# A fused attention and low-rank feed-forward layer: the low-rank term as a product of its own, and queries in 64-row products

## The chip, the cores and the metric

The kernel runs on one core of one Trainium2 chip. The metric is the device time of one execution in microseconds (us). Lower is better.

## What is computed

The input x has 2 sequences of 1024 tokens with 512 features. It is normalised over its features to xn. From xn come grouped-query attention s (32 query heads, 8 key and value heads, 16 features each, causal) and a gated feed-forward layer g. The output is x + s * g. Cut to what matters:

```python
q = xn @ Wq;  k, v = xn @ Wkv                    # 32 query heads, 8 groups
s = softmax(causal(q @ k.T) / sqrt(16)) @ v @ Wo + bo
def lora(x, w, a, b):                            # rank 16
    return x @ w.T + (x @ a.T) @ b.T
gate = lora(xn, gate_w, gate_a, gate_b)          # 512 -> 1376
up   = lora(xn, up_w, up_a, up_b)                # 512 -> 1376
g = silu(lora(silu(gate) * up, down_w, down_a, down_b))
out = x + s * g
```

All tensors are float32.

## The kernel before

**Split products.** A float32 factor is split into a rounded high part and a low part, both float32r, and a product is formed as high*high + high*low + low*high. `matmul_hi_lo` does that with three products over all 128 rows of the array (lines 289 to 291). Other places give each product only 64 rows: `hidden` (line 1018) and `changing_over` (line 1052) issue them in pairs, one in the upper half of the rows and one in the lower, each half into its own PSUM bank, and a second sweep (`cross`) goes over the same sum with the halves exchanged. A pair runs side by side. A profile row writes the rows and columns of the array that a product takes, as 128\*128, 64\*128 or 128\*32.

**Two programs woven into each engine's queue.** `attention()` runs in 16 rounds, one for each group and sequence, of 40 slots (`SLOTS`). A round has 48 score tiles `s` for the row maxima (line 1153, read by VectorE in `maximum`, lines 1730 and 1733; three banks), 40 transposed score tiles `st` (line 1172, two banks, one for each head of a pair), which ScalarE turns into `prob` by Exp (line 1449), causal masks by GpSimd (line 570), and context products `o` (line 1189). `background()` runs the rest: transposes of x (`turn`), projections (`proj`), values, the feed-forward units (`hidden`), then the down projection and the output. `interleave` hands out background work by steps: each unit has so many (`STEPS`), one step falls due per slot, and every engine follows the same count. `bank_order` is the order of the units. Two PSUM banks, `bank[0]` and `bank[1]`, serve the background; a unit takes one of them in turn, or both.

**Feed-forward weights.** For each block h of 128 hidden features (11 blocks, `NH`) and for gate and up (i = 0, 1), `fold(h, i)` transposes the raw weight (four products with the identity, line 993) and adds the low-rank product b*a into the same bank (four products, line 997). So the low-rank term goes into the weight. ScalarE rounds the result out of PSUM (`split_weight`, line 1278), VectorE subtracts for the low part (`low_weight`, line 1557). Then `hidden(h, c)` multiplies with the four chunks c of 512 tokens; ScalarE, VectorE and GpSimd form silu(gate)*up (lines 1289, 1571, 579, 581, 587). `fold_down` (lines 1032 and 1036) does the like for the down weights.

**Order in a period.** One h is a period of 40 slots in all queues: `hidden(h, 0)`, `hidden(h, 1)`, `fold(h + 1, 0)`, `fold(h + 1, 1)` (4 steps), one query projection of `AFTER` (4 steps), `hidden(h, 2)`, `hidden(h, 3)`. The last h has no folds.

**Start.** Before the first score tile stand eight turns, four projections (`LEADING`) and two values. During the first 40 slots, in which only `s` tiles and no Exp run, come the turns, projections and values of chunks 2 and 3, the first query projection of `AFTER` and `fold(0, i)`. Of the raw low-rank factors, `low_of_low_b` (line 1538) and `low_of_low_a` (line 1545) form low parts on VectorE, ahead of score maxima in its queue.

**Waits.** `scores_t` issues a pair of `st` products after one wait, which asks that both banks of the previous pair have been read by Exp.

## Time and profile before

| | us |
|---|---|
| median of 3 runs | 942.4 (938.22 to 943.74) |
| the profiled execution | 940.22 |
| its span, first to last instruction | 938.5 |
| TensorE busy | 894.9 (95%) |
| VectorE busy | 582.7 (62%) |
| ScalarE busy | 488.3 (52%) |
| GpSimd busy | 314.7 (34%) |
| transposes of `fold` (line 993), 88 products | median 273 ns |
| low-rank products of `fold` (line 997), 88 products | median 276 ns |

The span leaves 1.7 us of the profiled execution outside it. The profiled execution is one run; the median stands 2.2 us above it. PE is TensorE, DVE VectorE, ACT ScalarE, POOL GpSimd. Products overlap in the array, so the duration of one is longer than the distance to the next: the distances between starts say what a product takes of TensorE's time.

### The profile page before, as it was taken

The page shows a single profiled execution, that of the slowest core. Times are in us where ns is not written, and L with a number is a line of the kernel's source. Part 1 is how long each engine was busy: PE and PEld are TensorE (multiplying, and loading weights), DVE is VectorE, ACT ScalarE, POOL GpSimd, SP SyncE. Part 2 cuts the span into 40 slices and gives each one's busy share as a digit, 9 for nine tenths or more (in the row PEclk, how much of TensorE's full clock was granted, in tenths as well). Part 3 has the DMA queues.
Part 4 walks back from the last instruction along what each step waited for, and adds up shares of the span by engine and source line. Part 5 has one row for each costly group of instructions (what it writes and reads, how often), then busy time and mean ns, then how long its engine had stood idle before and what let it go on. Part 6 is the DMA issues. An engine that isn't in the chain of part 4 may idle for free.

```text
span 938.5 us, 21107 instructions
## 1 busy us (share of the span) xinstructions
PE 894.9 (95%) x8075; PEld 632.1 (67%) x8075; DVE 582.7 (62%) x1688; ACT 488.3 (52%) x990; POOL 314.7 (34%) x316
## 2 busy tenths in 40 slices
PE   3998999999999999999999999999899999999997
PEld 3755767676666666767666666654677777777885
DVE  6756666666666656566656565767666667660136
ACT  3513656565565656565656565656545455545211
POOL 4222235252525353535343443532011313130133
PEclk9979999999999999999999999997999999999999
DMA  9466343433334342424344434357475446434664
GB/s 292 160 197 186 103 131 97 120 98 113 111 104 122 93 135 72 141 68 138 80 121 107 120 89 134 80 141 209 143 221 158 155 142 178 153 110 123 214 209 141
DMA packets 133730, 129.20 MB, mean 138 GB/s; under 512 B 36176, under 2 KB 104368, under 8 KB 131360
## 3 DMA queue, kind: packets, MB, share of 16 engines
q1 hardware_dynamic: 133632, 127.87, 46.1%
q8 instruction: 65, 1.06, 0.5%
q14 instruction: 33, 0.27, 0.1%
HBM read 74.07 MB, written 53.22 MB: 136 GB/s over the span
## 4 chain that ended last, share of the span: by engine, by line
PE 88%; DVE 4%; ACT 2%; SPq 2%; issue 2%; DMA 2%; DVEq 0%; ACTq 0%
PE bank L1018 27%; PE o L1189 15%; PE bank L1052 12%; PE s L1153 10%; PE st L1172 8%; PE bank L289 4%; PE bank L290 4%; PE bank L291 4%; PE bank L993 1%; DMA ring<-in_L_attn_x 1%; PE bank L997 1%; ACT prob L1449 1%; SPq L933 1%; PE s L1160 1%; DVE junk L1730 1%
## 5 line engine op out<-in xcount | busy, mean ns | idle before, releaser
L1449 ACT ACTIVATE prob<-st 128x512 f32<-128x512 f32 (+1 forms) x640 | 323.2, 554 | 260.5 <-PE st L1172 260.0
L1730 DVE CUSTOM_DVE_ANT_0 junk<-s,mask 128x128 bf16<-128x128 f32 (+3 forms) x512 | 229.1, 487 | 67.2 <-PE s L1153 65.1
L1733 DVE TENSOR_REDUCE part_max<-s 128x1 f32<-128x512 f32 x256 | 164.1, 683 | 114.4 <-PE s L1153 114.3
L1153 PE MATMUL s<-k,q 64*128 64x512 f32 (+3 forms) x768 | 150.2, 378 | 10.7 <-DVE part_max L1730 5.3
L570 POOL TENSOR_SCALAR_AFFINE_SELECT prob<-prob 128x512 f32<-128x512 f32 x128 | 81.8, 651 | 218.4 <-ACT prob L1449 217.0
L1018 PE MATMUL bank<-x_hi,w_hi 64*128 64x512 f32 (+1 forms) x704 | 150.0, 412 | 2.5 <-DVE hid L1571 1.1
L1189 PE MATMUL o<-prob,v 128*32 128x512 f32 (+3 forms) x1536 | 145.0, 496 | 0.0
L1018 PE MATMUL bank<-x_lo,w_hi 64*128 64x512 f32 (+1 forms) x704 | 142.6, 391 | 0.0
L1018 PE MATMUL bank<-x_hi,w_lo 64*128 64x512 f32 (+1 forms) x704 | 142.1, 390 | 0.0
L1172 PE MATMUL st<-q,k 64*128 64x512 f32 (+3 forms) x768 | 130.3, 356 | 2.6 <-ACT prob L1449 1.8
L1052 PE MATMUL bank<-down_hi,late_context_hid_in 64*128 64x256 f32 x1056 | 113.3, 287 | 0.3 <-DVE y L1587 0.3
L1153 PEld LDWEIGHTS s<-k,q 64*128 64x128 f32 x768 | 78.7, 187 | 51.5 <-DVE part_max L1730 24.4
L579 POOL TENSOR_TENSOR tanh<-tanh,hid 128x512 f32<-128x512 f32 (+1 forms) x44 | 56.5, 1285 | 163.7 <-DVE hid L1571 163.7
L1052 PEld LDWEIGHTS bank<-down_hi,late_context_hid_in 64*128 64x128 f32 x1056 | 91.3, 188 | 16.1 <-issue 15.2
L1018 PEld LDWEIGHTS bank<-x_hi,w_hi 64*128 64x128 f32 (+1 forms) x704 | 69.2, 182 | 40.4 <-issue 30.6
L1172 PEld LDWEIGHTS st<-q,k 64*128 64x128 f32 x768 | 73.1, 186 | 29.0 <-issue 10.6
L1189 PEld LDWEIGHTS o<-prob,v 128*32 128x32 f32 x1536 | 39.7, 110 | 64.1 <-issue 58.0
L587 POOL TENSOR_TENSOR hid_lo<-hid,tanh_hid_hi 128x512 fp32r<-128x512 f32 (+1 forms) x44 | 56.8, 1292 | 72.0 <-ACT tanh_hid_hi L1306 72.0
L1052 PE MATMUL bank<-down_lo,late_context_hid_in 64*128 64x256 f32 x528 | 77.5, 281 | 0.1
L1018 PEld LDWEIGHTS bank<-x_lo,w_hi 64*128 64x128 f32 (+1 forms) x704 | 69.0, 182 | 12.5
L1018 PEld LDWEIGHTS bank<-x_hi,w_lo 64*128 64x128 f32 (+1 forms) x704 | 69.2, 183 | 7.8
L581 POOL TENSOR_TENSOR hid<-tanh,hid 128x512 f32<-128x512 f32 (+1 forms) x44 | 56.6, 1287 | 3.5
(148 smaller groups left out, 1088.7 us busy)
## 6 DMA issues: line engine op xcount, KB each, us to landing
late_context_hid_in<-scratch_hid SPq DMA_DIRECT2D x16, 1408.0 KB, 6.5
q<-scratch_q SPq DMA_DIRECT2D x60, 200.0 KB
scratch_hid<-tanh_hid_hi SPq DMA_DIRECT2D x40, 256.0 KB, 2.2
scratch_hid<-hid_lo SPq DMA_DIRECT2D x40, 256.0 KB, 2.5
scratch_o<-o_sb SPq DMA_DIRECT2D x32, 256.0 KB
scratch_q<-proj_hi SPq DMA_DIRECT2D x30, 256.0 KB
k<-scratch_k SPq DMA_DIRECT2D x30, 192.0 KB
x_again<-in_L_attn_x SPq DMA_DIRECT2D x16, 256.0 KB, 4.5
```

Of the source, the lines that this page charges most:

```text
L570: ins = pool.affine_select(out=blk, in_=blk, compare_op=ALU.is_ge, fill=0.0, base=0, pattern=[[0, REP], [1, P]], channel_multiplier=-1)
L579: pool.tensor_tensor(th[0:hp, n % 2], th[0:hp, n % 2], hid[0:hp, n % 2], ALU.mult).then_inc(tanh_used, 1)
L581: pool.tensor_tensor(hid[0:hp, n % 2], th[0:hp, n % 2], hid[0:hp, n % 2], ALU.add).then_inc(hid_done, 1)
L587: pool.tensor_tensor(hid_l[0:hp, n % 2], hid[0:hp, n % 2], hid_h[0:hp, n % 2], ALU.subtract)\
L1018: mm = pe.matmul(bank[i][0:hp, :], w_[half, h % 2, i, kt, 0:hp], x_[half, c, kt], start=not cross and kt == 0 and w_ is wh and x_ is xh, s ...
L1052: mm = pe.matmul(bank[i][:, COLUMNS[i]], lhs[half], rhs[half, COLUMNS[i]], start=not cross and n == 0 and m == 0, stop=cross == 1 and n == ...
L1153: pe.matmul(sb_[(p + odd) % S_BANKS][:, 0:wd], q[half, g % 2, h // 2, qt * P:(qt + 1) * P], k[half, g % 2, k0:k0 + wd], start=True, stop=T ...
L1172: mm = pe.matmul(st[odd][:, col:col + q1 - q0], k[half, i % 2, kt * P:(kt + 1) * P], q[half, i % 2, h // 2, q0:q1], start=True, stop=True)
L1189: mm = pe.matmul(ob[32 * h:32 * h + 2 * HD, q0 % C:q0 % C + q1 - q0], v[:, i % 3, kt].rearrange("p a e -> p (a e)"), prob[:, job % 3, h, c ...
L1449: nc.scalar.activation(prob[:, job % 3, h, 0:JOB_COLS[j]], st[at % ST_BANKS][:, 0:JOB_COLS[j]], ACT.Exp, scale=float(HD) ** -0.5).then_inc ...
L1730: ins = dve.tensor_tensor_reduce(junk[:, n % S_BANKS, 0:wd], bank_[:, 0:wd], mask[:, C - wd:C], 1.0, LOWEST, ALU.add, ALU.max, part[:, h, ...
L1733: ins = dve.tensor_reduce(part[:, h, qt, dst:dst + 1], bank_[:, 0:wd], AX.X, ALU.max)
```

## The change

- **The low-rank term leaves the weights.** `fold` is gone. The host hands over gate and up weights transposed, so that a raw tile arrives in the layout of `w_hi`. `low(i)` forms x*a for the gate and up factors together (32 columns) for two chunks at a time, eight float32 products, as i = 0 after the leading projections and i = 1 after the turns of chunk 3. The result is split and goes through DRAM (`store_x_a`, `load_x_a`) into `low_x_a`, whose rows 0 to 47 (gate) and 64 to 111 (up) hold high, low, high. In each `hidden(h, c)` one more pair of products, of 48 rows each, adds b times this to both banks (line 1108 of the changed kernel).
- **Weights are split from SBUF.** `round_weight` on ScalarE reads the raw tile; the subtraction moves from VectorE to GpSimd (`low_weight`). Both come two units before the block is used, beside `hidden(h, 2)` and `hidden(h, 3)`.
- **Query projections beside hidden units** (`BESIDE_HIDDEN`, 11 of them) go through `changing_over`: 48 products of 64 rows by 256 columns and both banks, in place of 12 of 128 rows by 512. They have 8 steps in place of 4 (the last one 4), so that a period keeps its 40.
- **Low parts of the small factors** leave VectorE: `low_of_low` on GpSimd takes the place of `low_of_low_b`; `low_of_low_a` has no successor.
- **One wait per score bank** in `scores_t`: the first product of a pair waits for its own bank, the second for its own.

Cut to its core:

```diff
+BESIDE_HIDDEN = AFTER[1:]
+QUERY_TILES = [[[0], [1], [2], [3]]] * 2
...
+QUERY_STEPS = [2 * KT] * (NH - 1) + [KT]
...
-STEPS = dict(turn=1, proj=KT, value=TT, fold=2, hidden=2 * KT, down_fold=2, rest=REST, down=NH + 1, out=KT)
+STEPS = dict(turn=1, proj=KT, value=TT, low=KT, hidden=2 * KT, down_fold=2, rest=REST, down=NH + 1, out=KT)
...
         yield "proj", c, blk
+    yield "low", 0, 0
     for c in range(2):
...
             yield "turn", c, k
+        if c == 3:
+            yield "low", 1, 0
...
-    for i in range(2):
-        yield "fold", 0, i
     for h in range(NH):
         for c in range(NCH):
             yield "hidden", h, c
             if c == 1:
-                if h + 1 < NH:
-                    for i in range(2):
-                        yield "fold", h + 1, i
                 yield "proj", *AFTER[SOON + h]
...
+EARLY = NUMBER_STEPS["proj", *AFTER[SOON - 1]] - FIRST_HIDDEN - LEAD
...
+            if kind == "proj" and (a, b) in BESIDE_HIDDEN:
+                return (p_left, BESIDE_HIDDEN.index((a, b)) + 1), (p_lo, projection(a, b) + 1)
...
+
+
+                pool.wait_ge(low_hi, 1)
+                pool.wait_ge(wq_lo, 3)
+                for half in range(2):
+                    at = slice(HALF_ROWS * half + 2 * R, HALF_ROWS * half + 3 * R)
+                    pool.tensor_tensor(b_gu[at], b_raw[at], b_gu[at], ALU.subtract).then_inc(low_lo, 1)
+                    pool.wait_ge(low_lo, half + 1)
+
+            def low_weight(h, i):
+                n, hp = 2 * h + i, rows[h]
+                pool.wait_ge(w_hi, n + 1)
+                pool.tensor_tensor(wl[:, h % 2, i, :, 0:hp], raw_tile(n)[:, :, 0:hp], wh[:, h % 2, i, :, 0:hp],
+                                   ALU.subtract).then_inc(w_lo, 1)
...
+                        low_of_low()
...
+                for i in range(2):
+                    low_weight(0, i)
...
                         done = at
                         if h or c:
                             low_hidden(*divmod(NCH * h + c - 1, NCH))
+                        if c >= 2 and h + 1 < NH:
+                            low_weight(h + 1, c - 2)
...
+            def load_x_a():
+                sp.wait_ge(x_a_stored, 2 * 2 * DMA)
+                for i in range(2):
+                    for j, part_ in enumerate((0, 1, 0)):
+                        row = HALF_ROWS * i + R * j
+                        sp.dma_start(low_x_a[row:row + R].rearrange("r (c t) -> r c t", c=NCH).bitcast(F32),
+                                     s["low"][part_, :, R * i:R * (i + 1)].rearrange("c r t -> r c t"))\
+                            .then_inc(x_a_landed, DMA)
...
-                    wait_filled(sp, ("fold", *divmod(before, 2)))
...
+                    sp.wait_ge(w_lo, before + 1)
...
                 out_ = take_bank(("proj", c, blk))
+                if (c, blk) in BESIDE_HIDDEN:
+                    cols = slice(blk * P, (blk + 1) * P)
+                    tiles = QUERY_TILES if (c, blk) != BESIDE_HIDDEN[-1] else OUT_STEPS
+                    yield from changing_over(
+                        ("proj", c, blk), lambda kt: [(wqh[:, kt, cols], xh[:, c, kt]), (wqh[:, kt, cols], xl[:, c, kt]),
+                                                      (wql[:, kt, cols], xh[:, c, kt])], tiles)
+                    return
...
-            def fold(h, i):
-                n = 2 * h + i
-                hp = rows[h]
-                pe.wait_ge(raw_landed[n % 8], DMA * (n // 8 + 1))
-                pe.wait_ge(low_lo, 2)
-                out_ = take_bank(("fold", h, i))
+            def low(i):
+
+
+                if i == 0:
+                    pe.wait_ge(low_landed, 2 * DMA)
+                pe.wait_ge(xT_copied, 2 * KT * (i + 1))
+                out_ = take_bank(("low", i, 0))
                 for kt in range(KT):
-                    pe.matmul(out_[:, kt * P:kt * P + hp], ring[0:hp, n % 8, kt * P:(kt + 1) * P], ident[0:hp, 0:hp],
-                              is_transpose=True, start=kt == 0, stop=False, skip_group_check=True)
-                yield 1
-                for kt in range(KT):
-                    mm = pe.matmul(out_[:, kt * P:kt * P + hp], a_gu[:, i, kt * P:(kt + 1) * P],
-                                   bT[:, i, h * P:h * P + hp], start=False, stop=kt == KT - 1, skip_group_check=True)
-                mm.then_inc(filled, 1)
-                yield 1
+                    for c in range(2):
+                        mm = pe.matmul(out_[GROUP * c:GROUP * (c + 1), :], a_raw[:, kt], xT[:, c, kt],
+                                       start=kt == 0, stop=kt == KT - 1)
+                    if kt == KT - 1:
+                        mm.then_inc(filled, 1)
+                    yield 1
 
...
+                        if kt == KT - 1 and not cross:
+                            if h == 0 and c == 0:
+                                pe.wait_ge(low_lo, 2)
+                                pe.wait_ge(x_a_landed, 6 * DMA)
+                            for i in range(2):
+                                at = head_rows(i, LOW_ROWS)
+                                mm = pe.matmul(bank[i][0:hp, :], b_gu[at, h * P:h * P + hp], low_x_a[at, c * C:(c + 1) * C],
+                                               start=False, stop=False)
                         if kt == KT - 1:
                             mm.then_inc(filled if cross else crossed, 1)
                         yield 1
...
-                if at >= ST_BANKS:
-                    pe.wait_ge(exp_done, at)
                 for kt, q0, q1, col in JOBS[j]:
                     for odd in range(2):
+                        if at >= ST_BANKS and kt == JOBS[j][0][0]:
+                            pe.wait_ge(exp_done, at + odd - 1)
...
+                if (c, blk) in BESIDE_HIDDEN:
+                    for i in range(2):
+                        ins = nc.scalar.activation(projected(n)[0][:, COLUMNS[i]], bank[i][:, COLUMNS[i]], ACT.Copy)
+                else:
+                    ins = nc.scalar.activation(projected(n)[0], bank_of(key)[:, :], ACT.Copy)
+                ins.then_inc(p_hi, 1)
...
-            def split_weight(h, i):
-                key = ("fold", h, i)
...
-                wait_filled(act, key)
...
-                nc.scalar.activation(wh[:, h % 2, i, :, 0:hp],
-                                     bank_of(key)[:, :].rearrange("p (k h) -> p k h", k=KT)[:, :, 0:hp],
-                                     ACT.Copy).then_inc(w_hi, 1)
+            def round_weight(h, i):
+                n, hp = 2 * h + i, rows[h]
+                if n == 0:
+                    wait_filled(act, ("value", NCH - 1, 0))
+                    act.wait_ge(xT_lo_late, 2 * KT)
+                act.wait_ge(raw_landed[n % 8], DMA * (n // 8 + 1))
+                nc.scalar.activation(wh[:, h % 2, i, :, 0:hp], raw_tile(n)[:, :, 0:hp], ACT.Copy).then_inc(w_hi, 1)
...
+                        yield WEIGHT_STEPS
+                        if c >= 2 and h + 1 < NH:
+                            round_weight(h + 1, c - 2)
...
-                dve.tensor_tensor(lo, bank_of(key)[:, :], hi, ALU.subtract).then_inc(p_lo, 1)
...
+                if (c, blk) in BESIDE_HIDDEN:
+                    for i, read in enumerate((p_left, p_lo)):
+                        dve.tensor_tensor(lo[:, COLUMNS[i]], bank[i][:, COLUMNS[i]], hi[:, COLUMNS[i]], ALU.subtract).then_inc(read, 1)
+                else:
+                    dve.tensor_tensor(lo, bank_of(key)[:, :], hi, ALU.subtract).then_inc(p_lo, 1)
...
-            def low_weight(h, i):
...
-                dve.wait_ge(w_hi, 2 * h + i + 1)
-                dve.tensor_tensor(wl[:, h % 2, i, :, 0:hp],
-                                  bank_of(key)[:, :].rearrange("p (k h) -> p k h", k=KT)[:, :, 0:hp],
-                                  wh[:, h % 2, i, :, 0:hp], ALU.subtract).then_inc(w_lo, 1)
...
+    for name in ("gate_w", "up_w"):
+        arrays[f"in_L0_ffn_{name}"] = np.ascontiguousarray(arrays[f"in_L0_ffn_{name}"].T)
```

The order of instructions shows two places. The first is TensorE's queue in the middle of a period, from the last context products ahead of the folds to the first work behind the first pair of `st` and `s` tiles. Before:

```order
L1189 MATMUL o<-prob,v 32x512 x3
L993 MATMUL bank<-ident,ring 128x128 [waits gate_read,up_read,low_lo_done,raw_landed4]
L993 MATMUL bank<-ident,ring 128x128 x3
L997 MATMUL bank<-bT,low_a 128x128 x4
L1172 MATMUL st<-q,k 128x512 [waits exp_done]
L1172 MATMUL st<-q,k 128x512
L1153 MATMUL s<-k,q 128x512 [waits s_read]
L1153 MATMUL s<-k,q 128x512
L993 MATMUL bank<-ident,ring 128x128 [waits gate_read,up_read,low_lo_done,raw_landed5]
```

And now (L1142 is the product of `changing_over`, L1260 and L1241 are the `st` and `s` tiles):

```order
L1277 MATMUL o<-prob,v 32x512 x3
L1142 MATMUL bank<-x_hi,wq_hi 128x256 [waits gate_read,up_read,wq_lo,xT_lo]
L1142 MATMUL bank<-x_hi,wq_hi 128x256
L1142 MATMUL bank<-x_lo,wq_hi 128x256 x2
L1142 MATMUL bank<-x_hi,wq_lo 128x256 x2
L1142 MATMUL bank<-x_hi,wq_hi 128x256 x2
L1142 MATMUL bank<-x_lo,wq_hi 128x256 x2
L1142 MATMUL bank<-x_hi,wq_lo 128x256 x2
L1260 MATMUL st<-q,k 128x512 [waits exp_done] x2
L1241 MATMUL s<-k,q 128x512 [waits s_read]
L1241 MATMUL s<-k,q 128x512
L1142 MATMUL bank<-x_hi,wq_hi 128x256 x2
```

Where two folds stood now stand 64-row products of the query projection, which has come forward by four steps; between context products and context products every product has 64 rows.

The second is GpSimd's queue between `finish` of one hidden unit and `finish` of the next (`tanh` and `hid` are its two products, `prob` the causal mask). Before:

```order
L587 TENSOR_TENSOR hid_lo<-hid,tanh_hid_hi 128x512 [waits hid_done,hid_hi_done]
L570 AFFINE_SELECT prob<-prob 128x4x128 [waits exp_done]
L579 TENSOR_TENSOR tanh<-tanh,hid 128x512 [waits up_read,gate_read]
L581 TENSOR_TENSOR hid<-tanh,hid 128x512 [waits tanh_used]
L570 AFFINE_SELECT prob<-prob 128x4x128 [waits exp_done]
```

And now:

```order
L621 TENSOR_TENSOR hid_lo<-hid,tanh_hid_hi 128x512 [waits hid_done,hid_hi_done]
L646 TENSOR_TENSOR w_lo<-ring,w_hi 128x512 [waits w_hi_done]
L604 AFFINE_SELECT prob<-prob 128x4x128 [waits exp_done]
L613 TENSOR_TENSOR tanh<-tanh,hid 128x512 [waits up_read,gate_read]
L615 TENSOR_TENSOR hid<-tanh,hid 128x512 [waits tanh_used]
```

A subtraction of a weight tile, which waits for ScalarE's rounding, stands behind `low_hidden`, ahead of a mask and of the next `finish`. It does so twice in each period but the last.

## Rows read from the trace of the kernel before

**Rows 1.** The page: head, busy time, and the maxima of 512 columns (busy, mean ns).
```profile
span 938.5 us, 21107 instructions
...
PE 894.9 (95%) x8075; PEld 632.1 (67%) x8075; DVE 582.7 (62%) x1688; ACT 488.3 (52%) x990; POOL 314.7 (34%) x316
...
L1733 DVE TENSOR_REDUCE part_max<-s 128x1 f32<-128x512 f32 x256 | 164.1, 683 | 114.4 <-PE s L1153 114.3
```

**Rows 2.** Waits of TensorE for Exp: us in total, times, longest.
```profile
PE st L1172 <- ACT prob L1449: 1.8, 4, 1.0
```

**Rows 3.** Stretches: us, busy of PE, PEld, DVE, ACT, POOL, then PEclk, DMA share, GB/s.
```profile
43.00:49.00 6.00, 3.96 (x24) 2.38 (x22) 5.92 (x10) 4.51 (x9) 4.25 (x3) 0.97 0.55 174
50.00:62.00 12.00, 12.00 (x30) 6.53 (x28) 5.29 (x21) 0.60 (x1) 2.69 (x3) 0.50 0.62 178
250.00:560.00 310.00, 308.99 (x2645) 208.29 (x2642) 197.41 (x608) 184.68 (x378) 129.23 (x127) 1.00 0.38 106
634.00:643.00 9.00, 7.37 (x47) 4.26 (x47) 7.42 (x24) 6.16 (x14) 5.60 (x6) 0.98 0.49 127
643.00:652.00 9.00, 9.00 (x49) 4.83 (x48) 6.95 (x27) 4.53 (x9) 0.63 (x1) 0.50 0.82 238
```

**Rows 4.** Timeline of TensorE, one period: start us, us, operation.
```profile
211.55 0.39 PE L1018 MATMUL bank<-x_lo,w_hi 64*128 64x512 f32 x2
211.78 0.39 PE L1172 MATMUL st<-q,k 64*128 64x512 f32 x2
...
214.27 1.92 PE L1189 MATMUL o<-prob,v 128*32 128x512 f32 x16
216.13 0.66 PE L993 MATMUL bank<-ident,ring 128*128 128x128 f32 x4
216.54 0.64 PE L997 MATMUL bank<-bT,low_a 96*128 96x128 f32 x4
217.12 0.50 PE L1172 MATMUL st<-q,k 64*128 64x512 f32 x2
217.45 0.40 PE L1153 MATMUL s<-k,q 64*128 64x512 f32 x2
...
219.66 0.50 PE L289 MATMUL bank<-x_hi,wq_hi 128*128 128x512 f32 x1
...
221.25 0.49 PE L1172 MATMUL st<-q,k 64*128 64x512 f32 x2
...
223.48 0.50 PE L1172 MATMUL st<-q,k 64*128 64x512 f32 x2
...
264.90 0.66 PE L993 MATMUL bank<-ident,ring 128*128 128x128 f32 x4
```

**Rows 5.** Timeline of TensorE: six pairs of 64x256 products, first, and what follows.
```profile
800.01 0.31 PE L1052 MATMUL bank<-wo_hi,ctx_hi 64*128 64x256 f32 x2
...
800.72 0.42 PE L1172 MATMUL st<-q,k 64*128 64x512 f32 x2
```

**Rows 6.** Timeline of ScalarE in the same period: two Exp.
```profile
217.72 1.08 ACT L1449 ACTIVATE prob<-st 128x512 f32<-128x512 f32 x2
```

**Rows 7.** Timeline of GpSimd: one subtraction of a 128x512 tile.
```profile
210.30 1.30 POOL L587 TENSOR_TENSOR hid_lo<-hid,tanh_hid_hi 128x512 fp32r<-128x512 f32 x1 [1.23 <-ACT tanh_hid_hi L1306]
```

**Rows 8.** Timeline of TensorE during fold_down: two neighbouring st pairs.
```profile
655.23 0.50 PE L1172 MATMUL st<-q,k 64*128 64x512 f32 x2 [0.18 <-ACT prob L1449]
...
656.89 0.50 PE L1172 MATMUL st<-q,k 64*128 64x512 f32 x2
```

**Rows 9.** Timeline of TensorE at the start: two score pairs that waited.
```profile
47.60 0.38 PE L1153 MATMUL s<-k,q 64*128 64x256 f32 x2 [1.17 <-DVE part_max L1730]
...
90.61 0.44 PE L1153 MATMUL s<-k,q 64*128 64x384 f32 x2 [2.37 <-DVE part_max L1733]
```

**Rows 10.** Timeline of VectorE at the start: the low parts of b and a.
```profile
43.72 3.51 DVE L1538 TENSOR_TENSOR bT<-prob,bT 32x688 fp32r<-32x688 f32 x3
...
88.53 1.21 DVE L1545 TENSOR_TENSOR low_a<-prob,low_a 32x1024 fp32r<-32x1024 f32 x1 [2.78 <-ACT low_a L1261]
```

221 lines of the change are left out of this document (118 added, 103 removed).

## The prediction

> **What bounds the kernel now.** I read the page first. TensorE is busy for 894.9 of 938.5 us, and VectorE, ScalarE and GpSimd are far behind it [rows 1]. Then the stretches: between 250 and 560 us, where `hidden`, `fold` and the query projections run beside attention, TensorE is busy for 308.99 of 310.00 us at full clock [rows 3]. The waits agree: `st` waits for Exp only 1.8 us in all [rows 2]. So in the middle what counts is how long TensorE's own queue takes, instruction by instruction. That is seen in the timeline, in distances between starts and not in durations. A pair of 64x512 products takes 0.23 us (211.55 to 211.78), and a pair of 64x256 half of it: six pairs take 0.71 us (800.01 to 800.72), 0.118 each [rows 4, 5]. Where a 64-row product follows one of 128 rows or stands ahead of it, the distance is 0.33 in place of 0.23 (217.12 to 217.45): a change between the two costs 0.10 on either side of it, and `fold` and the projections make such changes around each `st` and `s` pair [rows 4].
>
> There are two further losses in the rows. At the start score pairs wait for maxima (1.17 us at 47.60, 2.37 us at 90.61), while VectorE works on the low parts of b and a [rows 9, 10]. And the clock stands at 0.50, the lower of its levels (1.2 GHz), from 50 to 62 us and again from 643 to 652 us; before it fell TensorE had been busy for 3.96 of 6.00 and for 7.37 of 9.00 us [rows 3].
>
> **The change, part by part.**
>
> *The folds and the query projection in a period.* From the first fold to the first `st` pair behind the projection is 7.35 us (216.13 to 223.48) [rows 4]. In it lie two folds, twelve 128x512 products, three `st` pairs and three `s` pairs (512, 384 and 512 columns wide). In its place will stand 24 pairs of 64x256 at 0.118 = 2.84 us, three `st` pairs at 0.23 = 0.69, `s` pairs of 0.23 + 0.17 + 0.23 = 0.63, and 0.11 for the change behind the context products: 4.27 us. The `st` pair at 223.48 loses its 0.11 as well. That is 7.35 - 4.27 + 0.11 = 3.19 us, ten times: 31.9 us off. Slots keep their count, so nothing else moves.
>
> *What that stretch then waits for.* Two Exp take 1.08 us and begin 0.60 us behind their `st` pair (217.12, 217.72), 0.40 in the new stretch, where nothing is drained ahead of it (a row of such a pair lasts 0.39) [rows 4, 6]. So they end 1.48 us behind it, and with the hand-over about 1.5. The next pair comes 0.23 + 0.23 + 0.71 = 1.17 us behind the last. Its first product may now go with its bank free, but its second waits 0.35 us. From then on Exp runs without a gap and the pairs wait about 0.1 each. I take 0.5 us a period, 5.0 us given back. The floor is 0; the ceiling is the pace of `fold_down`, where neighbouring `st` pairs stand 1.66 us apart (655.23, 656.89) [rows 8]: 0.49 us more for each of three, 15 us in all. Nearest is the sum from Exp, since it is this stretch's own arithmetic.
>
> *The low-rank pair in each unit.* 44 units take one more pair of 512 columns: 44 x 0.23 = 10.1 us on, if 48 rows go like 64. For this speaks that the 96-row products of line 997 follow the 128-row ones of line 993 after 0.41 us, four transposes' own time, with nothing added (216.13, 216.54) [rows 4].
>
> *The last period* has no folds. Its twelve products take 4 x 0.79 = 3.18 us (219.66 to 221.25 is six of them with their first change), and some 0.8 us more of changes around them, against 2.84: 1.1 us off.
>
> *The first two folds* go: 0.99 us each (216.13 to 217.12) [rows 4], and 0.5 of changes: 2.5 us off.
>
> *Low parts at the start.* `low_of_low_a` held VectorE with its maxima behind it; the 2.37 us at 90.61 go. What replaces it in ScalarE's queue is two roundings, which no maximum waits for. With `low_of_low_b` gone (3.51 us for three of four), the 1.17 us at 47.60 go [rows 9, 10]. Off: 3.5 us. On GpSimd the same low parts stand ahead of the low parts of chunk 3, which are needed far later.
>
> *The products x*a.* Sixteen context products of 128\*32 take 1.86 us (214.27 to 216.13) [rows 4], so four 32-column tiles side by side take 0.465. A pair of `low` takes at least that, as its columns are streamed once: 8 x 0.465 = 3.7 us on. If the two don't run side by side it is 7.4. I take 3.7.
>
> *The clock at the start.* From 50 to 62 us all runs at half speed. If the clock holds, these 12 us take 6 or 7, as the maxima then set part of the pace. In the new order TensorE has less of a hole before it: the waits just named are gone, and `low(0)` pushes 1.9 us of dense work between the projections and the turns. I take it that the clock holds: 5.0 us off; bounds 0 and 6.
>
> *One wait per score bank* gives at most the 1.8 us of [rows 2], of which part is in places as tight as before: 0.5 us off.
>
> *At nothing:* ScalarE's rounding is the same 22 instructions. GpSimd gains 22 subtractions of 1.30 us (210.30) [rows 7], twice in a period of 48.8 us (216.13 to 264.90) [rows 4], in which it is busy for two fifths of the time (129.23 of 310.00) [rows 3]. Behind them in its queue stand a mask and `finish`. The weights are wanted only in the next period, and the tile loads on SyncE that wait for them stand half a unit later. A mask delayed by 1.3 us is wanted by a context product two slots after the last Exp of its job, some 2.4 us (48.8 / 40 each). If that cover is gone it costs up to 1.3 us at a mask, 26 us at most for 20 of them.
>
> **Sum:** -31.9 + 5.0 + 10.1 - 1.1 - 2.5 - 3.5 + 3.7 - 5.0 - 0.5 = -25.7 us, from the profiled execution's 940.2: **914.5 us**. The median of the runs is 942.4, so as a difference it is 2.7%.
>
> **The rivals.**
> - *The clock falls at the start as before.* For it: the hole between the values and the projections is still there, as ScalarE sets the pace of the turns. 5 us more: 919.5. I count it with the forecast's surroundings, chance 0.25.
> - *The query stretch is bound by Exp and maxima.* VectorE has 1.37 us for a pair of maxima of 512 columns (2 x 0.683) [rows 1], and TensorE only 1.17. Then it goes at the pace of `fold_down`, 15 us in place of 5: 924.5. For it: [rows 8] show just such a stretch. Against it: context products of 1.86 us stand on both sides, so VectorE begins with an empty queue. Chance 0.20.
> - *TensorE's columns alone decide.* No wait in the stretch: 909.5, and with some of the waits of [rows 2] gone 908. Chance 0.13.
> - *The 48-row pair doesn't go with its neighbours* (slower or equal). Each stands between 64-row products. If 48 rows are a setting of their own, each pays a change on both sides, 2 x 0.20, and its two products go one after the other, 0.23: 44 x 0.63 = 27.7 us on, 942. It decides from 25.7 / 44 = 0.58 us per unit. The Trainium skill (TensorEngine Tiling (Array Packing), "Key Properties") says "Changing tiling mode (not just tile) drains the TensorE" and lists row tiles of 128, 64 and 32 only; by that page 48 rows would be a 64-row tile, and 96 no other than 128, with which the 0.41 us above agrees. Chance 0.05.
> - *The clock falls in the query stretches* (slower). They hold half of the columns of a `hidden` stretch of as many slots, and the clock did fall in `fold_down`. At half speed for 9 us in each of ten periods [rows 3] it costs 45 us: 959. It decides from six periods. Against it: here TensorE would still work for 4.27 of 4.8 us. The Trainium skill (TensorE: Matmul & The Clock Gate, "What's actually happening") has the clock set by how busy the array has been; the two falls in the rows agree. Chance 0.04.
> - *GpSimd holds others up.* 20 masks delayed past their cover by the whole of a subtraction are the 26 us above, half of them 13: 927 to 940. For it: the subtraction stands straight ahead of a mask. Against it: no wait of TensorE for a mask is in the rows. Chance 0.05. The Trainium skill (SBUF — State Buffer, "SBUF: two separate sides") says that GpSimd and a VectorE operation with two SBUF inputs shut each other out for a whole instruction. By that rule the small split of the maxima, whose inputs are both in SBUF, could stand 1.3 us behind each of the 22 new subtractions, 28 us at the worst and next to nothing where the row maxima come back early; it speaks against the change, and no row here prices it.
>
> The forecast itself, with the clock held and short waits, has 0.28.
>
> **How the numbers follow.** A measurement of this kernel tells about 0.5% (5 us) from no change. From 908 to 925 lie the forecast, the first three rivals and most of what is between them: 0.86. The range that leaves out the two slow ends and takes in the doubled `low` (3.7 more) is 905 to 928. Faster by over 0.5% holds in all cases but the 48-row pair (same, 0.05) and the clock in each period (slower, 0.04): 0.91.
>
> **What would show it.** Six 64x256 pairs of the query projection in 0.71 us, and neighbouring `st` pairs there some 1.2 to 1.3 us apart; the stretch from the end of the context products to the next `st` behind the projection near 4.8 us. The pair of line 1108 between two 64x512 pairs at 0.23. A period of 48.8 - 3.2 + 0.5 + 0.9 = 47.0 us. No 2.37 us wait before the first hidden unit. PEclk at 1.00 between 50 and 62 us. The prediction fails if the 48-row pair shows gaps, if PEclk falls in each period, if VectorE or Exp hold the stretch, or if TensorE waits for masks.

## The result, and the profile after

The changed kernel takes 934.0 us (median of 8 runs, 931.33 to 935.92), the kernel before 940.8 in the same rounds (938.06 to 943.74): ratio 0.993, 95% interval 0.991 to 0.995. It is faster by 0.7%, 6.8 us, where I had forecast 2.7%, and the time lies above my range. The profiled execution has a span of 933.6 us against 938.5 [rows 1].

The page of the changed kernel, its head and busy time:

```profile
span 933.6 us, 21793 instructions
...
PE 885.7 (95%) x8415; PEld 641.2 (69%) x8415; DVE 576.6 (62%) x1674; ACT 488.9 (52%) x1002; POOL 345.4 (37%) x340
```

TensorE's busy time fell by 9.2 us, its instructions rose by 340. The stretches of [rows 3], and with them 102 to 108 us (columns: us, busy time of PE, PEld, DVE, ACT, POOL, then PEclk, DMA share, GB/s):

```profile
43.00:49.00 6.00, 5.84 (x44) 4.49 (x43) 5.05 (x20) 3.51 (x7) 1.75 (x2) 1.00 0.52 166
50.00:62.00 12.00, 10.38 (x53) 7.05 (x53) 9.73 (x26) 1.56 (x3) 9.73 (x5) 1.00 0.59 166
102.00:108.00 6.00, 2.93 (x13) 0.93 (x15) 0.51 (x4) 0.74 (x2) 1.23 (x2) 0.54 0.65 171
250.00:560.00 310.00, 308.62 (x2903) 219.46 (x2903) 201.10 (x623) 190.53 (x396) 148.73 (x143) 1.00 0.41 110
```

The clock holds from 50 to 62 us, as forecast. A new stretch is slow: from 102 to 108 us the granted clock is 0.54 and TensorE is busy for 2.93 of 6.00 us. The middle is as full as it was. What TensorE waits for in the first 125 us (total, times, longest), the first is in no such list of the kernel before:

```profile
PE s L1241 <- DMA q<-scratch_q: 6.6, 1, 6.6
PE s L1241 <- DVE part_max L1812: 2.9, 3, 1.5
...
PE bank L1077 <- ACT xT L1318: 1.3, 1, 1.3
```

The first row is the largest new thing in the trace. The chain that ended last, between 76 and 112 us (start us, us, what), leads back from it:

```profile
88.90 0.42 SPq L768
...
89.83 0.59 SPq L749
...
91.08 7.94 DMA scratch_k<-proj_hi
...
100.31 4.72 DMA q<-scratch_q
105.07 0.47 PE s L1241 x2
...
107.73 1.58 PE bank L1099 x6
```

And SyncE's queue in the same stretch:

```profile
83.37 1.31 SPq L749 DMA_DIRECT2D scratch_q<-proj_hi  x2
84.72 0.56 SPq L749 DMA_DIRECT2D scratch_q<-proj_lo  x1
85.33 4.46 SPq L768 DMA_DIRECT2D low_x<-scratch_low  x6
89.83 0.59 SPq L749 DMA_DIRECT2D scratch_k<-proj_hi  x1
90.46 0.57 SPq L749 DMA_DIRECT2D scratch_k<-proj_lo  x1
91.08 0.57 SPq L749 DMA_DIRECT2D scratch_k<-proj_hi  x1
99.07 0.79 SPq L949 DMA_DIRECT2D k<-scratch_k  x2
99.90 1.48 SPq L952 DMA_DIRECT2D q<-scratch_q  x4
```

The six loads of x times low_a (line 768) stand between the queries' stores and the keys' stores. The last store of keys lands 7.94 us after its issue begins, then k and q are loaded, then the scores of head group 1 can start, at 105.07 us. In the kernel before, SyncE's queue has the last store of keys and the load of k at:

```profile
83.95 0.68 SPq L692 DMA_DIRECT2D scratch_k<-proj_hi  x1
...
90.57 1.08 SPq L874 DMA_DIRECT2D k<-scratch_k  x2
```

There k is loaded 6.6 us behind the last store, here 8.0. The first hidden unit starts at 99.29 us in the kernel before and at 107.66 here.

The query stretch and the 48-row pair, TensorE's timeline, one period (to be held against [rows 4]):

```profile
221.07 1.92 PE L1277 MATMUL o<-prob,v 128*32 128x512 f32 x16
222.93 0.39 PE L1142 MATMUL bank<-x_hi,wq_hi 64*128 64x256 f32 x2
...
223.74 0.39 PE L1260 MATMUL st<-q,k 64*128 64x512 f32 x2
...
224.91 0.89 PE L1260 MATMUL st<-q,k 64*128 64x512 f32 x2
...
226.37 0.39 PE L1260 MATMUL st<-q,k 64*128 64x512 f32 x1
...
228.59 1.92 PE L1277 MATMUL o<-prob,v 128*32 128x512 f32 x16
...
234.08 0.43 PE L1108 MATMUL bank<-low_x,low_b 48*128 48x512 f32 x2
234.31 0.43 PE L1260 MATMUL st<-q,k 64*128 64x384 f32 x4
```

From the end of the context products to the next ones is 5.66 us (222.93 to 228.59), 8.02 before (216.13 to 224.15). The 48-row pair goes with its neighbours: 0.23 us from its start to the next.

### The profile page after: what moved, and what is told of

Read it like the earlier page. It is cut to its first block, busy times and chain, and to the rows that moved or that the text cites. A ratio compares the mean times of both kernels' runs of the same rounds, so it can differ in the third digit from the quotient of the medians.

```text
span 933.6 us, 21793 instructions
## 1 busy us (share of the span) xinstructions
PE 885.7 (95%) x8415; PEld 641.2 (69%) x8415; DVE 576.6 (62%) x1674; ACT 488.9 (52%) x1002; POOL 345.4 (37%) x340
## 4 chain that ended last, share of the span: by engine, by line
PE 86%; DVE 4%; DMA 3%; SPq 2%; ACT 2%; issue 2%; DVEq 0%; ACTq 0%
PE bank L1099 28%; PE bank L1142 15%; PE o L1277 14%; PE s L1241 9%; PE st L1260 8%; PE bank L306 3%; PE bank L307 2%; PE bank L308 2%; DMA sums<-scratch_o 1%; PE bank L1108 1%; PE bank L1077 1%; PE bank L1062 1%; SPq L968 1%; DMA scratch_k<-proj_hi 1%; PE bank L1122 1%
## 5 line engine op out<-in xcount | busy, mean ns | idle before, releaser
L1241 PE MATMUL s<-k,q 64*128 64x512 f32 (+3 forms) x768 | 157.6, 376 | 15.4 <-DMA q<-scratch_q 6.6
L1260 PE MATMUL st<-q,k 64*128 64x512 f32 (+3 forms) x768 | 141.7, 347 | 1.0 <-ACT prob L1543 0.5
L1241 PEld LDWEIGHTS s<-k,q 64*128 64x128 f32 x768 | 80.9, 187 | 54.0 <-DVE part_max L1809 22.7
L1142 PE MATMUL bank<-down_hi,late_context_hid_in 64*128 64x256 f32 x1056 | 114.2, 287 | 0.3 <-DVE y L1669 0.3
L1142 PEld LDWEIGHTS bank<-down_hi,late_context_hid_in 64*128 64x128 f32 x1056 | 93.3, 188 | 15.8 <-issue 15.0
L1260 PEld LDWEIGHTS st<-q,k 64*128 64x128 f32 x768 | 85.1, 187 | 19.6 <-ACT prob L1543 8.3
L1142 PE MATMUL bank<-down_lo,late_context_hid_in 64*128 64x256 f32 x528 | 79.1, 281 | 0.0
```

Of the source, the lines that this page charges most:

```text
L1142: mm = pe.matmul(bank[i][:, COLUMNS[i]], lhs[half], rhs[half, COLUMNS[i]], start=not cross and n == 0 and m == 0, stop=cross == 1 and n == ...
L1241: pe.matmul(sb_[(p + odd) % S_BANKS][:, 0:wd], q[half, g % 2, h // 2, qt * P:(qt + 1) * P], k[half, g % 2, k0:k0 + wd], start=True, stop=T ...
L1260: mm = pe.matmul(st[odd][:, col:col + q1 - q0], k[half, i % 2, kt * P:(kt + 1) * P], q[half, i % 2, h // 2, q0:q1], start=True, stop=True)
```

## Where the time went, by parts

I cut both programs in each period at the same slot: at the first product behind the context products that follow `hidden(h, 1)`. In the kernel before that is the first fold, in the changed kernel the first query product. (The first query product of the kernel before would be no such mark, since two folds stand ahead of it: 216.13 and 219.66 in [rows 4].) There are eleven marks; the first ten are nine periods apart. In us of the profiled executions, last column the mean of the nine:

| kernel | first mark | tenth mark | span | period |
|---|---|---|---|---|
| before | 118.67 | 557.50 | 938.5 | 48.76 |
| changed | 128.06 | 554.11 | 933.6 | 47.34 |

The program behind the first mark is 14.3 us shorter, the start 9.4 us longer. The middle gave 1.42 us a period, forecast 1.8 (48.8 to 47.0). From the tenth mark to the end it is 379.5 us against 381.0, 1.5 shorter, where my terms for that part make 2.4 (3.19 - 0.5 for the last stretch with folds, 1.1 for the last period, less six pairs of 0.23). Most of the miss is in the start. One execution says only so much of it: four kernels with the same start (the changed one and experiments 4, 8 and 11) reach the first mark at 128.06, 126.45, 125.28 and 125.32 us, mean 126.3; two with the start of before (that kernel and experiment 12) at 118.67 and 121.12, mean 119.9. So the start costs about 6.4 us more than before. Four terms of my sum (-2.5, -3.5, +3.7, -5.0) had taken 7.3 off it, and two 48-row pairs give 0.5 back. That is a miss of some 13 us, of 19 in all.

How the wait at the scores of head group 1 comes about is seen from the way of the last keys, in us of each profiled execution: when their low part is ready on VectorE, when their last store is issued, when the load of k is issued, when the scores start, and how long TensorE halts for them. The experiments are those of the next section.

| kernel | low part ready | last store | load of k | scores | halt |
|---|---|---|---|---|---|
| before | 82.69 | 83.95 | 90.57 | 97.84 | none |
| before, two waits (experiment 12) | 82.24 | 83.50 | 90.75 | 100.17 | none |
| changed | 88.38 | 91.08 | 99.07 | 105.07 | 6.55 |
| same start, experiment 4 | 85.63 | 88.33 | 96.43 | 102.86 | 7.12 |
| same start, experiment 8 | 84.62 | 87.60 | 95.46 | 101.44 | 6.68 |
| same start, experiment 11 | 84.72 | 86.80 | 95.61 | 101.56 | 6.70 |
| experiment 1 | 86.09 | 87.72 | 94.91 | 101.90 | 5.68 |
| experiment 2 | 85.29 | 87.40 | 95.68 | 102.13 | 6.72 |
| experiment 5 | 87.22 | 88.85 | 94.71 | 101.29 | 3.94 |
| experiment 9 | 80.96 | 83.33 | 90.26 | 96.33 | none |
| experiment 10 | 78.34 | 81.65 | 89.37 | 95.41 | 1.58 |

With the changed start (mean of its four kernels) k is loaded 6.0 us later than with the start of before (mean of two): the keys are ready 3.4 us later, their last store is issued a further 1.35 us later, and the load of k comes 1.25 us later behind it. TensorE for its part is through with its other work 3 us earlier than before, and halts.

## The experiments

All in rounds with the kernel before; ratios are to it, with their 95% interval. Its median was 940.8 us beside the changed kernel, 941.0 in experiments 1 to 4, 938.6 in 5 to 8 and 939.6 in 9 to 12, so between these groups the ratios compare better than the times.

**1. The six loads behind the last keys' stores.** The edit, in SyncE's order:

```diff
                     store_projection(*BESIDE[c])
-                    if c == 3:
-                        load_x_a()
                     yield STEPS["proj"]
                     store_projection(c, KEYS_BLOCK)
+                    if c == 3:
+                        load_x_a()
```

> One edit to the changed kernel: on SyncE the six loads of x times low_a stand behind the three stores of the last keys instead of ahead of them. Theory A (the order in SyncE's queue makes TensorE wait): the last keys are stored about 4.5 us earlier, TensorE's wait of 6.55 us for q<-scratch_q at 105.07 falls under 1.5 us, and with it the stretch at half clock behind it; the first hidden unit starts at 99 to 102 us instead of 107.66, and the time is 925 to 928.5 us (ratio to before 0.983 to 0.987). Rival B (the transfers themselves contend, whatever their order): the wait stays over 4 us and the time is 931 to 935. Rival C: the loads are now late for the first hidden unit, which waits over 2 us for them: 929 to 932.

Measured: 931.4 us, ratio 0.990 (0.988 to 0.992), against 0.993 for the changed kernel. SyncE's queue:

```profile
87.72 0.56 SPq L749 DMA_DIRECT2D scratch_k<-proj_hi  x1
88.34 5.58 SPq L768 DMA_DIRECT2D low_x<-scratch_low  x6
94.91 0.78 SPq L949 DMA_DIRECT2D k<-scratch_k  x2
```

TensorE, in the same kernel:

```profile
101.90 0.47 PE L1241 MATMUL s<-k,q 64*128 64x128 f32 x2 [5.68 <-DMA q<-scratch_q]
```

The last store is issued 3.4 us earlier (87.72 in place of 91.08), but 2.3 of that are the execution, in which the keys were ready earlier (86.09 in place of 88.38); the order in the queue gives 1.1. With the loads right behind it the store lands 7.13 us after its issue begins, and the wait is still 5.68 us. Rival B holds: the order of issue is a small part. The intervals of the two ratios overlap, and the first hidden unit starts at 104.49 us, where experiments 4, 8 and 11, which leave the start as it is, have 105.46, 104.03 and 104.16.

**2. A quarter of the products x times low_a.** The edit, in `low`:

```diff
-                    for c in range(2):
+                    for c in range(2 * (kt == KT - 1)):
                         mm = pe.matmul(out_[GROUP * c:GROUP * (c + 1), :], a_raw[:, kt], xT[:, c, kt],
-                                       start=kt == 0, stop=kt == KT - 1)
+                                       start=True, stop=True)
```

> The changed kernel with only one of the four row blocks of the product x times low_a (8 instead of 32 products; it leaves out three quarters of that sum, all else stays). Theory: these products are a plain cost on TensorE at the start, 0.9 us for a pair of products at full clock and more at half clock, so that 7 us go: first hidden unit at 100 to 101.5 us, time 926 to 928.5 (ratio 0.984 to 0.987), and the granted clock at 66 to 78 us is 1.0. Rival: the start is set by the chain of stores and loads behind SyncE, not by TensorE's own work: the wait for q<-scratch_q grows instead, and the time is 931 to 934.

Measured: 932.4 us, ratio 0.991 (0.988 to 0.993). Three quarters of 32 records at 0.23 us went, 5.6 us of TensorE's time at full clock, and 1.6 us were won, which the rounds hardly tell from nothing. The first hidden unit starts at 104.73 us, and the last keys are ready at 85.29, no earlier than with all the products (84.62 and 84.72 in experiments 8 and 11). The time is the rival's and the wait stays, 6.72 us, though it doesn't grow. But my theory also asked for a granted clock of 1.00 from 66 to 78 us, and it was 0.72, as in the changed kernel; in experiments 4, 8 and 11 it is 1.00 there. So part of the work that went may have come back as lower clock, and this run doesn't separate the two.

**3. The small subtraction on GpSimd moved.** The low parts of low_b are computed behind the last query weights (`low_of_low()` moved below `low_query_weights(3)`, with its own wait for them).

> The changed kernel with GpSimd's subtraction for the low parts of low_b (2 instructions of 3.16 us) moved from 53.6 us to behind the last query weights, at about 72 us. Theory (GpSimd holds VectorE up while it runs them): the third instruction of the split of the maxima, 3.12 us at 56.87 us, is under 0.5 us, and the 1.53 us wait of a score product at 61.33 is gone; time 932 to 933 (ratio 0.991 to 0.992), if no other VectorE instruction is held up at 72 to 79 us. Rival: the long subtraction has another cause and stays at about 3 us.

Measured: 931.7 us, ratio 0.990 (0.988 to 0.992). VectorE's timeline in the changed kernel:

```profile
56.66 0.17 DVE L1823 CAST neg_pad<-neg_max 128x16 fp32r<-128x16 f32 x1
56.87 3.12 DVE L1825 TENSOR_TENSOR neg_pad<-neg_max,neg_pad 128x16 fp32r<-128x16 f32 x1
```

GpSimd's beside it, the same kernel:

```profile
53.63 6.32 POOL L640 TENSOR_TENSOR low_b<-prob,low_b 16x1376 fp32r<-16x1376 f32 x2
```

And VectorE's in this one:

```profile
55.76 0.17 DVE L1823 CAST neg_pad<-neg_max 128x16 fp32r<-128x16 f32 x1
55.97 0.18 DVE L1825 TENSOR_TENSOR neg_pad<-neg_max,neg_pad 128x16 fp32r<-128x16 f32 x1
```

The same instruction on 128x16 elements takes 3.12 us or 0.18. In the changed kernel it ends at 59.99 us, and the two subtractions of GpSimd end at 59.95: it stood still for the whole of the second one. In all nine profiled kernels with the subtraction at this place one instruction of this split lasts 3.10 to 3.13 us; in the three with it moved neither does. In experiment 2 it was the one before, a copy, at 54.97, and GpSimd ended at 58.05. The Trainium skill (SBUF — State Buffer, "SBUF: two separate sides") says the pair of ports that the two share is locked for a whole instruction and the loser blocks; the trace agrees, with 3.12 against 0.18. I had cited this rule for the 22 new subtractions in the middle and not looked at the start, where a subtraction is 3.16 us long. TensorE's wait for maxima at 61.33 us fell from 1.53 to 0.32 (at 60.45). That is not yet time won: in experiment 8, with the subtraction at its old place, the same score product starts 4.65 us behind that copy on VectorE (55.88 to 60.53), and here 4.69 behind it (55.76 to 60.45), with a wait of 1.30 us for queries shortly before. So the hold-up is shown, and a cost to the program is not; the ratio overlaps with the changed kernel's.

**4. Query products of 128 rows again.** `BESIDE_HIDDEN = []`, with the same eight steps.

> The changed kernel with the ten query projections between the hidden units as products of 128 rows again, in the same eight steps. Theory (changes between 64-row and 128-row products and the time the array drains are what the 64-row products save): the stretch of 5.66 us becomes 6.5 to 7.0, 0.9 to 1.3 us in each of ten periods: 943 to 947 us (ratio 1.002 to 1.007). Rival (the 64-row products give nothing, since the time goes to waits for Exp and score banks): 933 to 937.

Measured: 940.9 us, ratio 1.000 (0.998 to 1.002). The stretch is 6.40 us (222.36 to 228.76) in place of 5.66, and the period 47.93 us in place of 47.34. The 64-row products give 0.6 to 0.7 us a period, 6 to 7 us in all; I expected 0.9 to 1.3, and the time lies between my range and the rival's. Their gain is clear, its size was too high.

**5. The six loads behind the values' stores too.** As in the first experiment, one place further down, so that k and q are loaded ahead of them.

> One edit to the changed kernel: the six loads of x times low_a (0.79 MB) stand in SyncE's order behind the last keys' and values' stores, and so behind the loads of k and q for the second head group too. Theory A2 (it is the bytes of the six loads in the DMA engines, and not only their 4.5 us of issuing, that hold up keys and queries; in the run with the loads right behind the keys the last store still took 6.6 us to land): that store lands in 3 to 4.5 us, the wait for q<-scratch_q falls under 1.5 us, the first hidden unit starts at 97 to 100.5 us, and the time is 924 to 927.5 us (ratio 0.982 to 0.9855). Rival: the landing is slow for another reason (other stores and loads in the same stretch): the wait stays over 4 us, 930 to 933.

Measured: 930.8 us, ratio 0.992 (0.990 to 0.994), which these rounds don't tell from the first experiment, nor from the changed kernel (0.991 to 0.995). The last store lands 5.80 us after its issue begins, in place of 7.94, and the wait is 3.94 us. The wait is 6.55 to 7.12 us in the four kernels with the loads ahead of the keys, and falls with each step by which the loads' 0.79 MB go back, to 5.68 and 3.94 in one execution each. But most of it stays: theory A2 is a part too. Left over is that the last keys are projected late and too little work stands behind them.

**6. Both.** Experiments 3 and 5 together.

> The edit of the run before and GpSimd's subtraction for low_b moved behind the last query weights, together. If the two losses at the start are independent and nothing new waits: 1.5 to 2.5 us below the run before, 922.5 to 925.5 (ratio 0.980 to 0.984), granted clock 1.0 at 66 to 78 us and at 96 to 108 us. Rival: they share one slack, and it is within 1 us of the run before.

Measured: 928.6 us, ratio 0.990 (0.988 to 0.992), span 927.0. The median is 2.1 us below the run before, as for independent losses, but above my range; the intervals overlap, so the sum is likely and not shown. The clock didn't come back everywhere: 0.72 from 66 to 72 us and 0.72 and 0.71 between 96 and 108.

**7. Without the 48-row pairs.**

```diff
-                            for i in range(2):
-                                at = head_rows(i, LOW_ROWS)
-                                mm = pe.matmul(bank[i][0:hp, :], b_gu[at, h * P:h * P + hp], low_x_a[at, c * C:(c + 1) * C],
-                                               start=False, stop=False)
```

> The changed kernel without the 44 pairs of 48-row products (it leaves out the low-rank term of gate and up, and keeps the work that prepares it). My price for them: 44 times 0.23 us, 10.1 us: 922.5 to 925.5 (ratio 0.981 to 0.984). Rival (the pair changes the array's mode or waits, and costs over 0.3 us each): under 921. Rival (the units wait for something else behind the first half, so the pairs are partly free): 927 to 931.

Measured: 923.4 us, ratio 0.983 (0.981 to 0.986), 10.6 us below the changed kernel (9.1 by the ratios); the period is 46.55 us, 0.79 less, so 0.20 for each of its four pairs. The price of 10.1 us was right.

**8. One wait for both score banks.**

```diff
+                if at >= ST_BANKS:
+                    pe.wait_ge(exp_done, at)
                 for kt, q0, q1, col in JOBS[j]:
                     for odd in range(2):
-                        if at >= ST_BANKS and kt == JOBS[j][0][0]:
-                            pe.wait_ge(exp_done, at + odd - 1)
```

> The changed kernel with one wait for both score banks of a pair again, as before the change. My price for that step is 0.5 us: 933.5 to 935.5, so no difference that five rounds can tell. Rival (where TensorE reaches the scores before Exp is done, in the query stretches, the first product of a pair fills 0.1 to 0.2 us each time): 936 to 939.

Measured: 938.1 us, ratio 0.998 (0.996 to 1.000), where the changed kernel has 0.993 (0.991 to 0.995). The rival holds. TensorE's waits for Exp from 125 us on (total, times, longest) in this kernel:

```profile
PE st L1260 <- ACT prob L1543: 9.1, 33, 1.0
```

The changed kernel:

```profile
PE st L1260 <- ACT prob L1543: 0.5, 1, 0.5
```

And one place in a query stretch with one wait:

```profile
222.91 0.28 PE L1142 MATMUL bank<-x_hi,wq_lo 64*128 64x256 f32 x2
223.42 0.50 PE L1260 MATMUL st<-q,k 64*128 64x512 f32 x2 [0.23 <-ACT prob L1543]
223.76 0.34 PE L1241 MATMUL s<-k,q 64*128 64x384 f32 x2
223.94 0.28 PE L1142 MATMUL bank<-x_hi,wq_hi 64*128 64x256 f32 x2
...
225.09 0.49 PE L1260 MATMUL st<-q,k 64*128 64x512 f32 x2 [0.29 <-ACT prob L1543]
```

The 0.23 us shown as a wait is not all: from the last query pair to the `st` pair is 0.51 us where 0.12 would do, as between two query pairs, and the pair loses 0.11 at its end. Three times a period this makes a stretch of 6.38 us (221.05 to 227.43) against 5.66. The `st` pairs stand 1.56, 1.67 and 1.67 us apart here (221.86, 223.42, 225.09, 226.76), the pace of `fold_down` in [rows 8].

**9. The second product of low_a behind the last keys.** On top of experiment 5, `low(1)` stands behind the projection of the last keys, on all engines, in place of ahead of the two projections:

```diff
-                    if c == 3:
-                        yield from low(1)
                     yield from project(*BESIDE[c])
                     yield from project(c, KEYS_BLOCK)
+                    if c == 3:
+                        yield from low(1)
```

> The changed kernel with the six loads behind the last values' stores as in the run before, and with the second product of x times low_a behind the projection of the last keys instead of ahead of the two projections (on all engines). Theory A3 (what binds is the chain from the last keys' projection over store and load to the first scores of head group 1, about 12 us, and TensorE has less work behind that projection than it had): the projection is ready 3 to 5 us earlier and the product covers the wait: the wait for q<-scratch_q is under 1 us, the wait for xT of 1.32 us is gone, first hidden unit at 98 to 100.5 us, 925.5 to 928.5 us (ratio 0.984 to 0.9875). Rival: the six loads become the late ones and the first half of the first hidden unit ends in a wait of over 2 us for low_x: 929 to 932.

Measured: 927.8 us, ratio 0.987 (0.984 to 0.990). TensorE's waits for loads in the start, and the scores of head group 1:

```profile
PE bank L1108 <- DMA low_x<-scratch_low: 2.4, 1, 2.4
PE s L1241 <- DMA q<-scratch_q: 2.1, 1, 2.1
```

```profile
96.33 0.33 PE L1241 MATMUL s<-k,q 64*128 64x128 f32 x2
```

The 2.1 us for queries lie at 58.62 us, in the first head group, where the other kernels wait up to 2.01 us too; the scores of head group 1 start at 96.33 without a wait. The first hidden unit starts at 97.79 us, ten earlier than in the changed kernel and six to eight earlier than in experiments 4, 8 and 11, and halts in its middle at 101.9 us for the loads, which land last. Both A3 and its rival show, and the time is that of A3: the chain of the keys is covered, and the loads are the late ones, for 2.36 us. Behind this wait the clock is at its lower level again: 64x512 pairs stand 0.43 us apart (105.47, 105.90) in place of 0.23.

**10. The same and the small subtraction moved.**

> The run before with GpSimd's subtraction for low_b behind the last query weights as well. 1.5 to 2.5 us below it if the two are independent: 923.5 to 926.5 (ratio 0.981 to 0.985); within 1 us of it if they share a slack.

Measured: 927.4 us, ratio 0.986 (0.983 to 0.989), span 924.8, first mark 120.16, period 47.27. It is within 0.5 us of the run before, as I gave for a shared slack; experiment 3 can't show a gain of its own for this move either, so what they share stays open. The unit still halts 1.83 us for the loads. This is the best version, 1.4% below the kernel before and 0.7% below the changed one. Its first mark is still no earlier than that of the kernel before (118.67, and 121.12 in experiment 12), where my sum had it 6.8 us earlier.

**11. Experiments 4 and 8 together.**

> The changed kernel with 128-row query products and one wait for both score banks, both undone together. Each alone costs 4 to 7 us. If they work only together (with one wait the faster stretch runs into Exp, with 128-row products Exp is never late): no more than either alone, 939 to 943 us (ratio 0.998 to 1.003), and hardly a wait of st for prob. If they add up: 944 to 948.

Measured: 942.4 us, ratio 1.003 (1.001 to 1.005). The two edits don't add up: 942.4 is within the 939 to 943 that I gave for that. TensorE waits for Exp only here and there:

```profile
PE st L1262 <- ACT prob L1545: 1.6, 3, 1.0
```

**12. One wait per bank in the kernel before.**

> The kernel before with nothing changed but one wait per score bank. If that step only pays where the query products are short: no difference (ratio 0.998 to 1.002). If it pays by itself: 3 to 6 us faster (0.9935 to 0.997).

Measured: 938.6 us, ratio 1.000 (0.997 to 1.002). The period is 48.75 us, as before.

The marks of the last group, which hold the middle apart from the start:

| kernel | first mark | tenth mark | period |
|---|---|---|---|
| before | 118.67 | 557.50 | 48.76 |
| before, two waits | 121.12 | 559.88 | 48.75 |
| changed, 128-row queries and one wait | 125.32 | 558.22 | 48.10 |
| changed, 128-row queries, two waits | 126.45 | 557.86 | 47.93 |
| changed, 64-row queries, one wait | 125.28 | 556.22 | 47.88 |
| changed | 128.06 | 554.11 | 47.34 |
| changed, no 48-row pairs | 124.92 | 543.90 | 46.55 |

Removing the folds gives 48.76 - (48.10 - 0.79) = 1.45 us a period. On the 48.10, the two waits alone give 0.17, the 64-row queries alone 0.22, both 0.76: they work together, and nearly half of what they give is there only with both.

## Why the prediction was wrong, step by step

- **The step that failed is the start: -2.5 for the first two folds, -3.5 for the low parts, +3.7 for the products x*a and -5.0 for the clock, where the start came out 6.4 us longer.** Under the products x*a I wrote only their columns on TensorE, and the folds I counted as pure gain. What that left out is the way of the last keys through DRAM. The change moves these keys back by `low(0)` and `low(1)`, puts six loads of 0.79 MB ahead of them in SyncE's queue, and takes two folds, 2 us of cover, from behind them. The result is a wait of 6.55 to 7.12 us in every kernel with this start, and the lower clock behind it. Of the 6.0 us by which k is loaded later, 3.4 are keys that are ready later and 2.6 the queue and the landing. Experiments 1, 5 and 9 move nothing but the order around it. Only the last, which puts `low(1)` behind the keys, takes the wait away: its ratio, 0.984 to 0.990, doesn't overlap with the changed kernel's 0.991 to 0.995. That the folds covered part of it is argued from their place; no run puts them back.
- **The products x*a were mis-sized:** forecast 3.7 us for both, measured 3.6 for the first alone. The products in the trace of the changed kernel (records, durations in ns, min/median/max):

```profile
L1077 PE MATMUL bank<-xT,prob x32: 592/604/1061, 34.2 to 75.9; 128*32 128x512 f32 x32
```

The products of the values, the other plain float32 ones:

```profile
L1062 PE MATMUL bank<-wkv,xT x128: 272/275/377, 37.8 to 93.0; 128*128 128x128 f32 x128
```

Each of the 16 products of 512 columns has two records, and a record lasts 0.604 us where a pass of 512 columns lasts 0.39: 0.21 more, which is 512 columns at 2.4 GHz. So a product here streams its columns four times. The records stand 0.23 apart, so the two tiles do run side by side, as I took it. I had taken the price from context products, whose operands are rounded to float32r, for a product of plain float32. The fitting row was in the kernel before, the products of the values:

```profile
84.87 2.05 PE L980 MATMUL bank<-wkv,xT 128*128 128x128 f32 x16
```

So 16 records of 128 columns take 2.05 us, 0.26 for a product's two, where 128 columns at 2.4 GHz are 0.053. The Trainium skill (FP8 and Floating Point Precision, "TensorE Precision Notes") gives true FP32 four passes through the array; the trace agrees. At half clock, as for part of `low(1)` in the changed kernel, the same takes longer still: eight of its records 3.63 us against 1.91 in experiment 5.
- **The clock at the start:** it held from 50 to 62 us, as I took it, but the 5.0 us were not won, since it was low elsewhere: 0.81 from 62 to 80 us and 0.54 from 102 to 108. The first belongs to this execution, for experiments 4, 8 and 11 have 1.00 there. The second stands in all of them (0.50 to 0.54), behind the wait for the keys. The fall that I priced varies too: with the start of before, experiment 12 has 0.72 from 50 to 62 us and 0.59 from 92 to 98. I had priced a fall as something that goes; it has to be asked where the next hole will be.
- **Low parts at the start:** the waits of [rows 9] went. "On GpSimd the same low parts stand ahead of the low parts of chunk 3, which are needed far later" looked at the queue behind them and missed VectorE beside them: a new wait of 1.53 us for maxima stands at 61.33. What it costs the program isn't shown (experiment 3).
- **Folds and query projection:** 24 pairs at 0.118 came as forecast (the first six in 0.81 with the change, six others in 0.71). The stretch is 5.66 us between context products, where my figures make 5.3 (8.02 - 3.19 + 0.5). The period gave 1.42 instead of 1.8, and this stretch is 0.33 of the difference.
- **What that stretch waits for:** I took 0.5 us a period, of waits. Without any the stretch would be 4.83 us by my figures (8.02 - 3.19). It is 5.66, so they are 0.83, and with one wait for both banks 6.38, so 1.55. In the changed kernel the list of waits shows only 0.5 us for the whole program, since TensorE rarely stands still as a whole. The time is in the pairs, whose two products no longer start together (226.37, one record in place of two).
- **One wait per score bank** was the worst-sized term of the middle: forecast 0.5 us in all, measured 0.54 a period and 4 to 5 us in the time, because I read its worth from the waits of the kernel before. There it is worth nothing (experiment 12), and with 128-row query products 0.17 a period. It is worth the 0.54 only in the short stretch that another part of the change makes.
- **The rivals:** the clock did fall at the start, elsewhere than before; the query stretch isn't bound by Exp or maxima at the pace of `fold_down` (its `st` pairs stand 1.17 and 1.46 us apart, not 1.66), but with one wait for both banks it is (experiment 8), and the 15 us of that rival fit the 1.55 a period; the clock stays at 1.00 in the periods. The time lies in the range that I gave the rival of GpSimd's masks, 927 to 940, and its cause is another. No rival had the way of keys and queries through DRAM.
- **The 48-row pair** was right in mechanism and size (10.1, measured 10.6). **GpSimd's 22 subtractions** cost TensorE next to nothing in the middle: no wait for a mask, none for weights. They do hold VectorE up, as my last rival had it: between 125 and 560 us its 18 small subtractions of the maxima (line 1825) take 15.4 us in place of 12.0. But TensorE's waits for maxima from 125 us on are 4.5 us against 4.1, so the maxima come early enough. **The last period** was to give 1.1 us less. Its stretch took 5.22 us (601.67 to 606.89) against 5.41 (606.84 to 612.25), 0.2 less: it ends in a wait for VectorE's low part of the projection, 1.22 us against 0.90.

What stays open: why one execution of the same start takes up to 2.8 us more than another (128.06 against 125.28), of which the clock is the visible part; and how the 2.6 us of queue and landing divide, since the loads' issues and their bytes move together in experiments 1 and 5.

## What to carry to other kernels

When work is taken out of TensorE's queue, look for the transfer that it covered: keys and queries were on their way through DRAM beneath the two folds. When work is put in, look for what is sent on its way behind it: here the place of `low(1)`, ahead of the last keys or behind them, weighed more than the issues and the bytes of the loads. A new bounce through DRAM is costed in three places, the issues in the queue that it stands in, the bytes beside what is landing, and the store that now waits behind both. A wait that costs nothing in the kernel before may be worth several microseconds in the stretch that the change creates, so edits that work on the same stretch are priced together. And a price is taken from a row with the same operand type.

## What the runs showed of the hardware

- A VectorE instruction of 0.17 us on small SBUF tiles (128x16) took 3.10 to 3.13 us in all nine kernels in which GpSimd began a subtraction of SBUF tiles of 3.1 us just before it, and ended within 0.05 us of it.
- 48-row products go in a row with 64-row ones, 0.23 us a pair, without a break.
- From the issue of the last keys' store to the load of k behind its landing it took 6.6 and 7.3 us with the start of before, 7.9 to 8.8 with 0.79 MB of loads issued just ahead of it, 7.2 with them just behind it, and 5.9 with them after its landing.
- TensorE was at its lower clock level behind a wait of 2.4 us (experiment 9: 0.72 from 102 to 108 us) and of 6.55 us (the changed kernel: 0.54). Behind the 2.37 us of [rows 9] it stayed at 1.00 from 92 to 98 us.
